# Delta heads: gate projection behind the queries, other projection banks, weight turns moved, second merge level as pairs of 32x32 products

## The reference, cut to what matters

```
q, k, v = (silu(causal_conv4(x @ W.T)) for W in (Wq, Wk, Wv));  q, k = l2norm(q), l2norm(k)
g = exp(-exp(A_log) * softplus(x @ Wa.T + dt_bias));  beta = sigmoid(x @ Wb.T)
for each token t:                       # S is a 128x128 state per batch row and head
    S = g_t * S + outer(k_t, beta_t * (v_t - g_t * (S.T @ k_t)))
    o_t = S.T @ q_t
o = rmsnorm(o) * norm_w * silu(x @ Wg.T);  y = o @ Wo.T
```

## Time and profile before

| | us |
|---|---|
| median of 3 runs | 3416.99 |
| profiled execution, own time | 3415.16 |
| its span | 3413.4 |
| PE busy | 3180.1 (93%) |
| DVE busy | 2191.9 (64%) |
| ACT busy | 1898.9 (56%) |
| POOL busy | 1672.6 (49%) |

### The profile page before, as it was taken

One profiled execution on the slowest core, in us unless ns is written; L12 is line 12 of the kernel. 1 busy time (PEld: TensorE's weight loads), 2 busy tenths in 40 slices (PEclk: granted clock), 3 DMA queues, 4 the chain that ended last, 5 costly groups with the idle time before them and its releaser, 6 DMA issues. The chain is left out here.

```text
span 3413.4 us, 60026 instructions
## 1 busy us (share of the span) xinstructions
PE 3180.1 (93%) x18834; PEld 2544.9 (75%) x18834; DVE 2191.9 (64%) x4849; ACT 1898.9 (56%) x4657; POOL 1672.6 (49%) x3107
## 2 busy tenths in 40 slices
PE   6899999999999999999999788799979999998998
PEld 3688888888888888888878555488866777776543
DVE  5577777777777777777653488765547567574432
ACT  3677777777777777777532377644445445363111
POOL 2777787777788777778630000145534002011322
PEclk9899999999999999999999999999989999999999
DMA  4222222222222222222353333423351222211854
GB/s 113 63 73 69 59 69 62 73 68 67 74 55 73 62 73 68 65 76 53 97 176 92 115 142 142 177 87 103 115 174 57 68 69 69 93 65 53 271 99 56
DMA packets 432408, 310.47 MB, mean 91 GB/s; under 512 B 130496, under 2 KB 347456, under 8 KB 431072
## 3 DMA queue, kind: packets, MB, share of 16 engines
q1 hardware_dynamic: 423792, 289.57, 28.8%
q0 software_dynamic: 8432, 18.88, 2.8%
HBM read 177.97 MB, written 130.43 MB: 90 GB/s over the span
## 5 line engine op out<-in xcount | busy, mean ns | idle before, releaser
L631 PE MATMUL gd_PJ<-xn_lead,gd_w_rest 128*128 128x512 f32 x1024 | 421.3, 411 | 0.5 <-DVE gd_w_rest L786 0.5
L631 PE MATMUL gd_PJ<-xn_lead,gd_w_lead 128*128 128x512 f32 x1024 | 403.0, 394 | 0.0
L631 PE MATMUL gd_PJ<-xn_rest,gd_w_lead 128*128 128x512 f32 x1024 | 401.9, 393 | 0.0
L1079 POOL TENSOR_TENSOR gd_prod<-gd_L,gd_T 32x14 f32<-32x14 f32 (+6 forms) x896 | 324.8, 362 | 70.4
L1082 POOL TENSOR_TENSOR gd_T<-gd_T,gd_prod 32x14 f32<-32x14 f32 (+6 forms) x896 | 311.6, 348 | 71.6 <-POOL gd_prod L1079 2.5
L793 DVE SCALAR_TENSOR_TENSOR gd_conv<-gd_pre,gd_cur_a,gd_conv 128x512 f32<-128x512 f32 x384 | 301.8, 786 | 13.3 <-ACT gd_conv L958 2.9
L631 PEld LDWEIGHTS gd_PJ<-xn_lead,gd_w_lead 128*128 128x128 f32 x1024 | 193.8, 189 | 43.4
L631 PEld LDWEIGHTS gd_PJ<-xn_lead,gd_w_rest 128*128 128x128 f32 x1024 | 194.4, 190 | 38.5 <-DVE gd_w_rest L786 0.9
L631 PEld LDWEIGHTS gd_PJ<-xn_rest,gd_w_lead 128*128 128x128 f32 x1024 | 194.6, 190 | 35.3
L932 DVE SCALAR_TENSOR_TENSOR gd_og<-gd_B,ptab,gd_gate 128x512 f32<-128x512 f32 x64 | 48.1, 751 | 243.8 <-PE gd_B L645 243.8
L2619 ACT ACTIVATE sa_E<-sa_B,sa_nmax 128x512 f32<-128x512 f32 (+3 forms) x256 | 131.3, 525 | 131.4 <-DVE sa_nmax L2756 127.2
(11 more groups left out here) (476 smaller groups left out, 8620.3 us busy)
## 6 DMA issues: line engine op xcount, KB each, us to landing
expert_rows<-xt_blank SPq DMA_DIRECT2D x16, 2112.0 KB, 7.3
turned_queries_keys<-f_wq SPq DMA_DIRECT2D x16, 1280.0 KB, 6.0
x_wo<-decay_sums SPq DMA_DIRECT2D x64, 256.0 KB, 3.7
triangles<-gd_Lo SPq DMA_DIRECT2D x64, 256.0 KB, 3.5
gd_W<-turned_image SPq DMA_DIRECT2D x64, 256.0 KB
gd_T<-inverse_image SPq DMA_DIRECT2D x64, 256.0 KB
gated_outputs<-gd_og SPq DMA_DIRECT2D x64, 256.0 KB, 2.8
go_ogt<-gated_outputs SPq DMA_DIRECT2D x16, 1024.0 KB, 5.9
```

The lines of the kernel that those rows point to most:

```text
L631: mm = pe.matmul(bank, w_parts[wp][:, j, k, :], rhs, start=(k == 0 and wp == 1), stop=(k == KT - 1 and wp + xp == 0))
L1079: nc.gpsimd.tensor_tensor(prod[:, rows, 0:j], L16[:, rows, j:j + 1].to_broadcast(shape), T16[:, j:j + 1, 0:j].to_broadcast(shape), ALU.mul ...
```

## The change

The gate projection moves from the end of PE's slot to right behind the query projection. The banks become queries and values 1, keys and gate 0. Weights are turned as keys c = 1, gate and queries c = 2, values c = 3. `spread_rows(1)` and `merge(1)` become eight products of 32x32 each (four batch rows x two diagonal blocks) whose results lie in two PSUM banks, and their copies on DVE are two instructions of 32 partitions without a mask. T is no longer turned whole; a new tile `inv` takes two smaller transposes right behind `merged(0)`. On DVE two query taps come ahead of `masked(1)` and the key-norm chain goes behind `merged(2)`; on ACT the gate's silu goes behind the copy of the queries and the square root behind the queries' silu.

```diff
-        W_BANK = (0, 0, 1, 1)
+        W_BANK = (0, 1, 1, 0)
+        W_TURN = (1, 4, 3, 2)
...
@@ PE
+                    elif l == 1:
+                        pe.wait_ge(og_ready, n + 1)
+                        pe.sem_inc(blocks_open, 1)
+                        for b in range(B):
+                            for q, bank in PAIRS:
+                                lo, hi = slice(q, q + SIDE), slice(q + SIDE, q + 2 * SIDE)
+                                mm = pe.matmul(bank[lo, b, 0:SIDE], Lo_c[hi, b, lo], W_c[hi, b, hi], start=True, stop=True)
+                        mm.then_inc(y_sum, 1)
...
+                    if l == 1:
+                        pe.sem_inc(blocks_open, 1)
+                        for b in range(B):
+                            for q, bank in UPPERS:
+                                at = slice(q, q + SIDE)
+                                mm = pe.matmul(bank[at, b, 0:SIDE], inv[at, b, q:q + SIDE], Y[at, l % 2, b, 0:SIDE], start=True, stop=True)
+                        mm.then_inc(wup, 1)
...
                     project(JQ, c1, q_proj)
-                if back and more and c == 1:
-                    pe.wait_ge(k_pre, n + 3)
-                    turn_weights(i + 1, JK)
+                    if has2:
+                        pe.wait_ge(k_pre, n + 3)
+                    elif back:
+                        pe.wait_ge(g_silu, n + 2)
+                    pe.wait_ge(w_copied, h1 * 4 + W_TURN[JG])
+                    project(JG, c1, g_proj)
+                if back and more and c == CH - 1:
+                    pe.wait_ge(q_pre, n + 2)
+                    turn_weights(h1, JV)
...
                     project(JV, c1, v_proj)
+                if back and more and c in (1, 2):
+                    pe.wait_ge(g_silu, n + 3)
+                    turn_weights(i + 1, JK if c == 1 else JG)
...
                     turned(Bk[5], k_m, k_turned)
-                    pe.wait_ge(q_pre, n + 2)
-                    pe.wait_ge(w_copied, h1 * 4 + JG + 1)
-                    project(JG, c1, g_proj)
+                if back and more and c == 2:
+                    pe.wait_ge(v_pre, n + 4)
+                    turn_weights(i + 1, JQ)
...
@@ DVE
                 def turned_blocks():
                     dve.wait_ge(w_ready, n * NM + 1)
-                    nc.vector.transpose(T_c, W_c).then_inc(t_next, 1)
+                    nc.vector.transpose(inv[0:TOP, :, 0:TOP], W_c[0:TOP, :, 0:TOP])
+                    at = slice(2 * SIDE, 3 * SIDE)
+                    nc.vector.transpose(inv[at, :, at], W_c[at, :, at]).then_inc(inv_ready, 1)
...
                     merged(0)
+                    turned_blocks()
                 if has2:
                     tap(n + 2, par, PK, cur_k, (2,), k_tap)
...
-                if back:
-                    turned_blocks()
-                    masked(1)
                 if has1:
...
-                    tap(n + 1, parm, PQ, cur_a, (0,), q_tap)
+                    tap(n + 1, parm, PQ, cur_a, (0, 1), q_tap)
+                if back:
+                    masked(1)
+                if back and more and c == CH - 1:
+                    rest_weights(h1, JV)
+                if back:
+                    merged(1)
+                    turned_corner()
+                if has1:
+                    tap(n + 1, parm, PQ, cur_a, (2,), q_tap)
+                if back:
+                    masked(2)
...
                     nc.vector.tensor_reduce(kss[:, :], diag[:], AX.X, ALU.add).then_inc(k_len, 1)
                 if back:
-                    turned_corner()
-                    masked(2)
-                if has1:
-                    tap(n + 1, parm, PQ, cur_a, (1, 2), q_tap)
+                    merged(2)
                 if has2:
                     dve.wait_ge(k_root, n + 3)
...
-                if back and more and c == CH - 1:
-                    rest_weights(h1, JG)
+                if back and more and c in (1, 2):
+                    rest_weights(i + 1, JK if c == 1 else JG)
                 if has1:
                     dve.wait_ge(v_halo, n + 2)
...
@@ ACT
                     copy_pre(parm, PQ, JQ, cur_a, q_pre)
+                    act.wait_ge(g_proj, n + 2)
...
+                    nc.scalar.activation(gate[:, parm, :], PJ[:, W_BANK[JG], :], ACT.Silu).then_inc(g_silu, 1)
...
                     silu(PQ, qT[:, parm, :], q_silu)
+                if has2:
+                    act.wait_ge(k_len, n + 3)
+                    nc.scalar.activation(klen[:, :], kss[:, :], ACT.Sqrt).then_inc(k_root, 1)
...
                     copy_pre(parm, PV, JV, cur_a, v_pre)
+                if back and more and c in (1, 2):
+                    lead_weights(i + 1, JK if c == 1 else JG)
...
-                if has1:
-                    act.wait_ge(g_proj, n + 2)
-                    nc.scalar.activation(gate[:, parm, :], PJ[:, W_BANK[JG], :], ACT.Silu).then_inc(g_silu, 1)
+                if back and more and c == 2:
+                    lead_weights(i + 1, JQ)
```

More of the change, by code:

```diff
@@ L672, in merge @@
                         pe.wait_ge(p_ready, n + 1)
-                    else:
[L674 to L678, removed]
-                if back and more and c == CH - 1:
-                    pe.wait_ge(g_silu, n + 2)
-                    turn_weights(h1, JQ)
+                        each(half[3], tiles(T_c), [Y[:, l % 2, b, :] for b in range(B)], wup)
+                        return
+                    pe.wait_ge(inv_ready, n * (NM - 1) + l)
+                    if l == 1:
[5 more added lines that the diff above has]
+                        mm.then_inc(wup, 1)
+                    else:
+                        each(half[3][0:TOP], [inv[:, b, 0:TOP] for b in range(B)], [Y[:, l % 2, b, :] for b in range(B)], wup)
                 if back:
@@ L857, in slot @@
                     dve.wait_ge(q_pre, n + 2)
-                    tap(n + 1, parm, PQ, cur_a, (0,), q_tap)
-                if back and more and c == 1:
-                    rest_weights(i + 1, JK)
+                    tap(n + 1, parm, PQ, cur_a, (0, 1), q_tap)
[6 more added lines that the diff above has]
+                    turned_corner()
+                if has1:
+                    tap(n + 1, parm, PQ, cur_a, (2,), q_tap)
+                if back:
+                    masked(2)
                 if has2:
@@ L920, in slot @@
                         nc.vector.tensor_copy(S[:], Bk[1][:, :, :]).then_inc(s_ready, 1)
-                if back and more and c == 2:
-                    rest_weights(i + 1, JV)
                 if has1:
@@ L971, in slot @@
                     copy_pre(par, PK, JK, cur_k, k_pre)
-                if back and more and c == CH - 1:
-                    lead_weights(h1, JQ)
                 if back:
@@ L986, in slot @@
                     copy_pre(parm, PQ, JQ, cur_a, q_pre)
-                if back and more and c == 1:
-                    lead_weights(i + 1, JK)
-                if has2:
-                    act.wait_ge(k_len, n + 3)
-                    nc.scalar.activation(klen[:, :], kss[:, :], ACT.Sqrt).then_inc(k_root, 1)
+                    act.wait_ge(g_proj, n + 2)
+                    if back:
+                        act.wait_ge(og_ready, n + 1)
+                    nc.scalar.activation(gate[:, parm, :], PJ[:, W_BANK[JG], :], ACT.Silu).then_inc(g_silu, 1)
+                if back and more and c == CH - 1:
+                    lead_weights(h1, JV)
                 if back and c > 0:
@@ L1000, in slot @@
                     silu(PQ, qT[:, parm, :], q_silu)
-                if back and more and c == CH - 1:
-                    lead_weights(h1, JG)
+                if has2:
+                    act.wait_ge(k_len, n + 3)
+                    nc.scalar.activation(klen[:, :], kss[:, :], ACT.Sqrt).then_inc(k_root, 1)
                 if has1:
@@ L1018, in slot @@
                     silu(PV, vT[:, :], v_silu)
-                if back and more and c == 2:
-                    lead_weights(i + 1, JV)
                 if has3:
```

98 lines of the change are left out of this document (47 added, 51 removed).

## The result

The changed kernel took 3539.91 us (median of 4 runs, 3539.30 to 3545.48), the kernel before 3416.16 us (4 runs, 3413.04 to 3425.02). The ratio is 1.0362, 95% interval 1.0340 to 1.0383. The forecast was 3518 us, range 3440 to 3590: time, sign and range held. The steps behind it held only in part, and that is the larger part of what follows.

A forecast was written before the change was run, and what follows sets the result against it. PE and a second loop through DVE's `qss`, POOL's solve and the image were taken as tied. Terms of 2.79 + 0.35 + 3.5 + 0.2 = 6.84 us a head, 15 times, added 103 to 3415: 3518 us, range 3440 to 3590.

The forecast's parts named there:

- step 3: M1 to M2: late key copy, then taps and query copies ahead of `masked(1)`, delay `merge(1)`; +3.5 us per head.
- Steps 1 and 4: 1: gate projection lengthens S1 to M1, +2.79 us a head; 4: M2 to M3 grows at most +0.2.
- a rival at 0.27: PE's idle gaps also drop its clock to 1.2 GHz; 3567 us if once per head; chance 0.27.
- the rival's dearer case: The clock falls twice per head, behind waits ahead of `merge(1)` and at S1: 3617 us; rival's chance 0.27.
- step 2: M3 to S1: key-norm chain adds 0.94 us, `rest_weights` leaving takes off 0.60; +0.35, to 35.83 us.
- POOL's route: From M3 through `qss`, POOL's list, the 16.38 us solve, spreading and loading of the image to S1: 35.5 us.
- the 6.12 us behind it: Spreading and loading the image between the solve's end and S1, read from the earlier trace as 6.12 us.
- The loop I reasoned with: M3, value taps, `qss`, POOL, image, S1, then PE's list back to M3; claimed tied with PE.
- step 5: The 32x32 products: four groups a head on the loop, between -2.4 and +1.2 us, taken as 0.
- my own signs of being wrong: Period below 99.65 us, PE busy throughout, c = 2 key copy before M1 + 13, product groups far from 0.9 us.

The follow-up runs named there:

- a2: Changed kernel with POOL's copy of `cur_k` at the start of slot c = 2, ahead of decay arguments and solve; 3511.88 us, ratio 1.0277.
- a1: Changed kernel with DVE's `masked(1)`, `merged(1)` and `turned_corner` ahead of all query taps but the first; 3508.66 us, ratio 1.0265.
- a3: Changed kernel with the edits of a1 and a2 together; 3471.08 us, ratio 1.0153.
- a6: a3 with `rest_weights(JQ)` of c = 3 ahead of the first key tap on DVE; 3449.57 us, ratio 1.0100.
- a7: a6 with POOL's `under` and `above` moved behind the solve in c = 0 alone; 3397.32 us, ratio 0.9943.
- b1: Kernel before with the 32x32 products alone (with their masks, copies, part transposes), nothing moved; 3428.36 us, ratio 1.0040.
- a4: a3 with POOL's `under` and `above` moved behind the solve in every slot; 3495.03 us, ratio 1.0232.
- b2: Kernel before with only POOL's `under` and `above` moved behind the solve; 3451.07 us, ratio 1.0104.
- b6: b1 with `merged(1)` ahead of the key norm's `diag` on DVE, plus the POOL edits of a2 and a7; 3389.20 us, ratio 0.9924.
- a5: a4 with `rest_weights(JQ)` of c = 3 ahead of the first key tap on DVE; 3429.57 us, ratio 1.0033.

## Why the prediction was right, and where it was wrong

The segments of a head, mean of eleven heads, before and after, with the forecast:

```
          before   after   change   forecast
S1 to M1   13.71   16.24    +2.53      +2.79
M1 to M2   24.85   30.00    +5.15      +3.5
M2 to M3   25.65   25.99    +0.34      +0.2
M3 to S1   35.50   35.43    -0.07      +0.35
sum        99.71  107.66    +7.95      +6.84
```

**Right: the chain in chunk 2 (step 3).** The keys are copied at M1 + 13.2 (13.8 foretold), `merge(1)` starts at M1 + 22.25 (1376.58 - 1354.33; 22.5 foretold), and `cur_k` is what holds it (a2). The query taps ahead of `masked(1)` are the other link: with them behind it chunk 2 gets as short (a1). Steps 1 and 4 came within 0.3 us.

**Missing from the sum: the clock,** which I had left to a rival at 0.27. From `merge(1)` to M2 the forecast had 5.8 us; it took 7.8 on average, against 5.5 in a1 and a2, where the clock does not fall there. From `merge(1)` to M0 chunk 0 took 6.5 against 4.7 in the one head without a fall. Together 4.1 us a head, 62 in all, is the clock's. It fell twice per head, as the rival's dearer case had it, but one fall cost 2 us and not 3.3, since it lasted 3.4 or 6.8 us and covered idle time too. The Trainium skill, TensorE: Matmul & The Clock Gate, section HAM oscillation, describes a wait in every pass of a loop that throttles every pass; the trace agrees, 23 falls in 12 heads, and the waits beside them in the head shown were 2.13 and 2.32 us.

**Failed: the cause in step 2.** I had S1 wait some 4 us for the image, with POOL's route as in the earlier trace rows. From the solve's first operation to its end it took 14.0 us (1424.23 to 1438.19) and not 16.4, so with the 6.12 us behind it the image was there 2.3 us ahead of S1 (1.6 on average). The solve is thus the term that was too large: between 200 and 1500 us it took 14.06 us on average in this place, where it took 16.40 before. Why it got shorter no run isolates; in a3 it took 15.4. PE stood still ahead of `merge(1)` of chunk 0 instead, 2.1 us and 0.7, and lost the rest to the clock. M3 to S1 came out the same for other reasons. The step overlooked that chunk 0 has the same queue of taps ahead of `masked(1)`, and that its key taps now run against `under` and `above` (3.31 us for two). Without the clock the segment is 1.9 us shorter than before. The loop I reasoned with is real and stands right behind: a1, a3 and a6 show it (M3 to S1 is 35.2 us in a3, 35.83 foretold), and a7 all but frees it.

**Right by accident: the products at 0 (step 5).** PE does save 0.33 us a group; two groups a slot make 0.7. b1 shows that PE waits 0.7 us a slot more than before for `merged(1)`, whose two narrow copies on DVE (0.57 us, where one took 0.41) stand behind the query tap and `diag` and come no earlier. I had bounded PE's cost and not asked who is late next. Groups far from 0.9 us were one of my own signs of being wrong, and that sign came.

So the sum: 62 us of clock that the forecast left out, some 48 that it had too much (34 in M3 to S1, 10 in M1 to M2, 4 in S1 to M1; each difference times 15). With 2 us in M2 to M3 that makes 16 of the 22 us by which the forecast is off; the rest lies outside the eleven heads. An error of 22 us in 124 is thus partly luck: two errors of opposite sign.

## What to carry to other kernels

Before work is moved out of a stage, look at what fills the idle time of the other engines there: DVE's wait ahead of `og` was where POOL's long operations ran almost for nothing. In a4 and b2, where they moved in every slot, the new place cost more than the loop gained; in a7 and b6, where they moved in one slot of four, it did not. When one engine is made faster at a point, read off the queue of the engine that must answer it; in b1 a saving on PE of 0.33 us a group turned into waits, and the clock fell behind some of them. Two ties stand one behind the other in such a kernel, so undo stalls together (a1, a2, a3) before judging any of them.

## What the runs showed of the hardware

A tiny DVE operation with two SBUF inputs (`twice`, 128x8) stood for 3.20 us beside three POOL operations in a row of 0.84, 1.25 and 1.25 us (b2): it ended with the last of them and not between two. Over 200 to 1500 us its mean rose from 241 to 646 ns. One with a single SBUF input (`klen`, 128x4) stood in the same way, 2.55 us in a4. The half clock came in stretches of 3.4 or 6.8 us beside PE waits of 1.6 to 1.7 us (b1, in 6 of 13 heads), 2.1 to 2.3 us (the changed kernel, nearly every time) and 3.3 to 4.0 us (a3); a5, a7 and b6 had none between 200 and 1500 us. Eight 32x32 products, sixteen instructions, took 0.37 us together from start to start, 0.023 each instruction.
